# Products of constants between the masked scores of an attention stage

## The reference

```python
def _L3_gnn_ref(x, Wq, Wk, Wv, Wo, edge_index):          # 4 heads of 8
    src, dst = (edge_index[0], edge_index[1])
    q = (x @ Wq).reshape(N, N_HEADS, D_HEAD)
    k = (x @ Wk).reshape(N, N_HEADS, D_HEAD)
    v = (x @ Wv).reshape(N, N_HEADS, D_HEAD)
    scores = jnp.einsum('ehd,ehd->eh', q[dst], k[src]) * inv_sqrt_d
    m = jax.ops.segment_max(scores, dst, num_segments=N)
    e = jnp.exp(scores - m[dst])
    denom = jax.ops.segment_sum(e, dst, num_segments=N)
    msg = jax.ops.segment_sum(e[:, :, None] * v[src], dst, num_segments=N)
    attn_out = msg / jnp.maximum(denom, 1e-16)[:, :, None]
    return x + attn_out.reshape(N, N_HEADS * D_HEAD) @ Wo
```

## Time and profile before

| | us |
|---|---|
| median of 3 runs | 4871.88 |
| lowest, highest run | 4849.11, 4895.27 |
| span of the profiled execution, first to last instruction | 4857.7 |
| TensorE matmul busy | 2328.2 (48%) |
| VectorE busy | 1913.1 (39%) |
| ScalarE busy | 475.2 (10%) |
| GpSimd busy | 2571.2 (53%) |

### The profile page before, as it was taken

The page is one execution under the profiler, slowest core; times in us unless marked ns, Lnnn a source line. Parts: engine busy times, 40 slices in busy tenths (PEclk is TensorE's granted clock), DMA queues, the critical chain, the costliest instruction groups (busy, mean ns, idle before and its releaser), DMA issues. The chain is left out here.

```text
span 4857.7 us, 64843 instructions
## 1 busy us (share of the span) xinstructions
PE 2328.2 (48%) x20169; PEld 1793.5 (37%) x20302; DVE 1913.1 (39%) x6164; ACT 475.2 (10%) x1072; POOL 2571.2 (53%) x2544
## 2 busy tenths in 40 slices
PE   1300002332363232335556489888888455565562
PEld 0100002333343332334555355555555344344441
DVE  8000001111121111144545466665665455555557
ACT  0000000000000000000000022222222111111110
POOL 4777775666626666644554444444443444444440
PEclk9555555555555555555656699999998556656655
DMA  3211111000020000010000100000000000000010
GB/s 89 62 7 7 7 7 48 12 11 12 11 72 12 11 11 12 12 19 14 15 15 14 12 9 8 8 8 7 8 7 5 19 15 15 16 14 16 15 15 4
DMA packets 122759, 82.94 MB, mean 17 GB/s; under 512 B 75092, under 2 KB 109016, under 8 KB 122456
## 3 DMA queue, kind: packets, MB, share of 16 engines
q0 software_dynamic: 80160, 46.17, 8.2%
q1 hardware_dynamic: 42552, 36.17, 2.6%
HBM read 54.41 MB, written 27.29 MB: 17 GB/s over the span
## 5 line engine op out<-in xcount | busy, mean ns | idle before, releaser
L598 POOL DMA_INDIRECT rel_rows<-message_table,rel_index x880 | 842.5, 957 | 519.0 <-issue 277.0
L630 PE MATMUL rel_acc<-rel_rows,rel_onehot 128*128 128x32 f32 x1760 | 393.6, 372 | 872.4 <-issue 582.9
L630 PEld LDWEIGHTS rel_acc<-rel_rows,rel_onehot 128*128 128x128 f32 x1760 | 402.5, 324 | 863.5 <-issue 863.2
L1002 POOL DMA_INDIRECT flow_x<-node_table,flow_index x440 | 424.6, 965 | 548.5 <-DVE flow_index L1017 440.4
L1357 POOL DMA_INDIRECT att_kv_rows<-kv_table,att_index x440 | 421.0, 957 | 508.9 <-DVE att_index L1368 380.3
L362 POOL DMA_INDIRECT sorted_edges<-scatter_rows,scatter_index x425 | 505.4, 1189 | 131.7 <-issue 128.8
L1139 PE MATMUL flow_acc_bwd<-flow_onehot_j,flow_by_q 128*128 128x309 bf16 (+1 forms) x2508 | 557.5, 337 | 8.8 <-issue 0.4
L798 POOL DMA_INDIRECT sum_rows<-node_table,sum_index x320 | 326.3, 1020 | 295.1 <-DVE sum_index L821 195.6
L609 DVE COPY rel_index<-message_indices 128x8 uint32 x110 | 22.2, 202 | 1051.7 <-remote 956.1
L860 PE MATMUL p_sum_picked<-sum_h_parts,sum_source_onehot 128*128 128x96 bf16 x3000 | 250.6, 260 | 209.7 <-issue 204.1
L831 DVE TENSOR_SCALAR sum_source_onehot<-sum_sources,sum_node_numbers 128x384 bf16<-128x384 f16 x1000 | 235.7, 314 | 289.1 <-PE p_sum_picked L860 148.8
(11 more groups left out here) (248 smaller groups left out, 3861.8 us busy)
## 6 DMA issues: line engine op xcount, KB each, us to landing
message_table<-message_rows SPq DMA_DIRECT2D x50, 320.0 KB, 2.1
rel_rows<-message_table,rel_index POOLq DMA_INDIRECT x880
flow_x<-node_table,flow_index POOLq DMA_INDIRECT x440
att_kv_rows<-kv_table,att_index POOLq DMA_INDIRECT x440
sorted_edges<-scatter_rows,scatter_index POOLq DMA_INDIRECT x425
sum_rows<-node_table,sum_index POOLq DMA_INDIRECT x320
sorted_edges<-records SPq DMA_DIRECT2D x1, 4400.0 KB, 12.0
records<-sorted_edges SPq DMA_DIRECT2D x1, 4400.0 KB, 13.1
```

Source lines behind the costliest of these rows:

```text
L598: pool.indirect_dma_start(out=rows[b][:, t, :], out_offset=None, in_=table, in_offset=bass.IndirectOffsetOnAxis(ap=ibuf[b][:, t:t + 1], ax ...
L630: last = pe.matmul(acc[:, bass.ds(col, F)], hot[b][:, t, :], rows[b][:, t, :], start=False, stop=True, skip_group_check=True)
L1002: pool.indirect_dma_start(out=X[b][:, t, 0:F], out_offset=None, in_=d["nodes"], in_offset=bass.IndirectOffsetOnAxis(ap=ibuf[b][:, t:t + 1] ...
```

## The change

A function stay_busy issues one product on constants: the moving operand is 256 columns of att_pick, the stationary one the first 96 rows of the bfloat16 identity, and the result goes to the bank of p_att_parts, at times at which nobody reads that bank. No instruction waits for it, and it waits for no other engine. In each step it is called 15 times: after every masked_scores and before every one but the first.

```diff
+                    def stay_busy():
+
+                        pe.matmul(pP[:].bitcast(F32)[:, 0:BANK // 2], s["identb"][0:3 * G * HEADS, :], pick[:, 0:2, :],
+                                  start=True, stop=True, skip_group_check=True)
+
...
                     def step(i, k):
                         for t in range(G // 2):
+                            if t:
+                                stay_busy()
                             stage(masked_scores, i, k, 2, t)
+                            stay_busy()
                             if t == G // 2 - 1:
                                 stage(pick_maxima, i, k, 3)
                             stage(pick_q, i, k, 1, (2 * t, 2 * t + 1))
                         for t in range(G // 2, G):
+                            stay_busy()
                             stage(masked_scores, i, k, 2, t)
+                            stay_busy()
                             if t == G // 2 + 1:
                                 stage(turn_onehots, i, k, 0)
                         stage(add_up, i, k, 3)
```

## The result

The changed kernel took 4963.53 us (median of five runs, 4958.92 to 4997.24), the kernel before 4871.88. The ratio is 1.0206, 95% interval 1.0167 to 1.0245: slower, by 92 us in the medians, where 143 were forecast. The time lies inside the range. The profiled run is the slowest of the five (4997.24, span 4995.4); against the profiled span before it is 137.7 us longer, and 16 of those lie in stages that the change does not touch, ahead of the attention stage, whose first gather starts at 3821.6 instead of 3805.4. From its first to its last gather that stage takes 1037.5 us instead of 920.9, 117 more.

The account below looks back on a forecast made before the run. Bound: a ring of waits in the attention stage, with TensorE's signals held while gathers run. 52 steps at +2.78 us give +145 on the 4857.7 us span, 5002; plus 14 for timed runs, about 5015 us, range 4865 to 5080.

Parts of the forecast that it names:

- What bounds the kernel: Attention stage: no engine is full; a ring of waits of 16.6 us, 11.5 of them the gathers and the hold.
- The cliff: Attention step: pick_maxima ending 2.40 instead of 2.15 us after the first gather puts the next gathers at 19.72, not 16.58.
- the hold: Attention stage: TensorE's signals are held back while gathers run; att_gap follows pick_maxima by 5 us instead of 0.03.
- (1): Each added 256-column product takes TensorE 0.21 us at 1.2 GHz, 0.11 at 2.4; 3.2 or 1.7 us a step.
- (2): Seven products ahead of pick_maxima's signal: it ends 3.7 us after the first gather at half clock, 1.8 to 2.35 at full.
- (3): Four products between turn_onehots and add_up: first mask product only 1.35 us ahead of gathers, so late steps make late steps.
- (4): Four products between pick_maxima and turn_onehots: idle time, no cost; if products trickle, 0.85 us on the path.
- (5): Full clock on TensorE ends pick_maxima 0.63 us earlier and shortens transposes; taken as hidden and counted as nothing.
- The sum: Attention stage: 52 steps at 19.72 instead of 16.94 us, +145 us, about 5015 us in all, +3.0%; chance 0.50.
- No change: Rival: full clock before the first mask product keeps steps at 16.6 us; 4872, up to 10 more; chance 0.22.
- faster: Rival: clock stays at 2.4 GHz, TensorE's work on the ring shortens 1.2 us a step, 62 us: 4810; chance 0.11.
- Slower still: Rival: everything behind the hold trickles and four products come on the path, 20.7 us a step: about 5068; chance 0.17.

Follow-up runs that it names:

- e1: Kernel before plus only the seven added products between the first mask product and pick_maxima, on the first chip: 4032.82 us, ratio 1.002.
- e4: Kernel before, no product added, VectorE's index copy moved ahead of the split of the maxima so gathers start earlier, on the first chip: 4023.45 us, ratio 1.0004.
- f2: Kernel before plus four 512-column products, all ahead of turn_onehots, on a chip with late signals: 4812.73 us, ratio 1.0014.
- f1: The whole change again, unaltered, against the kernel before on the same chip: 4915.01 against 4801.32 us, ratio 1.0216.
- g1: Kernel before plus only the seven added products ahead of pick_maxima, on a chip with late signals: 4853.93 us, ratio 1.0121.
- g2: Kernel before plus only the last eight added products, from behind pick_maxima to add_up, on a chip with late signals: 4890.65 us, ratio 1.0213.
- g3: Kernel before, no product added, index copy ahead of the split of the maxima so gathers start earlier, on a chip with late signals: 4848.81 us, ratio 1.0099.
- g4: Changed kernel with VectorE's one-hots moved ahead of att_gap: 4852.05 us, ratio 1.012 to the kernel before.
- h1: Kernel before, no product added, with VectorE's one-hots moved ahead of att_gap: 4912.5 against 4877.55 us, ratio 1.007.
- e2: Kernel before plus only the last eight added products, from behind pick_maxima to add_up, on the first chip: 4025.33 us, ratio 1.0009.
- e3: Kernel before plus four 512-column products, all ahead of turn_onehots, on the first chip: 4026.57 us, ratio 1.0013.

## Why the prediction was right, and where its size was off

**What bounds the kernel: right.** The signals are held while gathers run one behind the other, but not within GpSimd's pause, and not at all in the first set of runs (e1 to e4).

**The cliff: right in effect, a staircase in fact.** It was put between 2.15 and 2.40 us for the end of pick_maxima. The traces of before and f2 have 90 regular steps; 83 of them by the start of its last product, 0.17 us ahead of its end (the other seven are earlier):

```
last product of pick_maxima   steps   att_gap: least / median / most   next gathers, mean
+1.5 to +1.8                   18      7.07 /  7.21 /  8.64            16.51
+1.8 to +2.1                   34      5.67 /  7.20 / 10.75            16.65
+2.1 to +2.4                   20      7.09 /  8.63 / 11.47            17.43
+2.4 to +3.0                    4     10.66 / 11.37 / 11.44            19.20
above +3.0                      7     11.35 / 11.48 / 12.06            19.47
```

The signal comes mostly at 7.1, 7.8, 8.6, 9.9, 10.7 or 11.4 us (in five steps at 5.7). Up to 8.7 us a later signal costs next to nothing, since the gathers bound the step, at 16.5 us in the mean; beyond 9.5 the next gathers stand 7.97 us behind att_gap (standard deviation 0.2; before, after, f1, f2, g1 and g2 agree within 0.03), 7.40 in g3, whose indices come earlier, 6.95 in g4 and h1 with the one-hots out of the way. And att_gap is at 11.3 to 11.7 us in most late steps, 1.7 us behind the end of the last gather (9.7): the hold lasts little longer than the gathers. So a late step costs up to 2.9 us and hardly more, which is the ceiling that g1 and g2 show.

**(1) The price of a product: right, and beside the point.** At 2.4 GHz the next product starts 0.11 us behind an added one, at 1.2 GHz 0.22 (taken: 0.11 and 0.21). f2, e2 and e3 show no such price in the time, and e1 at most 0.4%.

**(2) Seven ahead of pick_maxima: right in kind.** Forecast from the first mask product to the end of pick_maxima: 4.4 to 4.9 us at full clock; the step above has 4.35 (just below, at the lower price of issue alone). Alone (g1) they decide by the clock, as written: late at half clock, over the edge or not at full.

**(3) Four between turn_onehots and add_up: right, and the larger part.** Forecast: first mask product 1.35 us ahead of the gathers; measured 1.33 in the step above, 1.44 in the mean, 1.44 with the last eight alone, which cost the whole 2.1%. That the late state feeds itself holds: 47 of 47 regular steps are late. The four steps with GpSimd's pause take 15.4 to 18.3 us, which the prediction did not look at.

**(4) Four in the idle time: right for usual steps (f2).** In late ones they trickle with the rest, the case that the prediction named. No run took them apart there; h1 shows that work behind the held signal can delay it, but the signal of a late step is at its ceiling already.

**(5) The clock counts nothing: wrong in g1, right for the whole.** The full-clock share of the stretch from the first mask product to pick_maxima rose from 0.39 to 0.67, and with the last eight in place no clock saves the step.

**The sum: the term that was mis-sized is 52 x (19.72 - 16.94).** It took one late step, that of the earlier trace rows, for all. A late step measured 19.53 in the mean, 19.42 in f1, and the four steps with GpSimd's pause are shorter; 52 steps average 19.16, so the term is 52 x 2.22 = 115 us and not 145 in the profiled runs, and 52 x (18.96 - 16.97) = 103 between f1 and f2, on one chip, where the timed medians stand 102 apart. The stage was put at about 1010 us and took 985. The timed medians stand 92 apart and not 138 like the profiled spans, since the profiled run of the changed kernel was its slowest, 34 us above its median, and the profiled span before lay 14 us below its own; 16 us of the 138 lie ahead of the stage.

**The rivals.** No change and faster both fell: the clock did rise, and neither left the steps at 16.6 us nor shortened them. Slower still fell too: 20.7 us a step was put on products on the path behind the signal, and the ceiling forbids it. By the Trainium skill, page "SBUF — State Buffer", section "Who interferes with whom", TensorE waits on nobody, said there of SBUF's ports, which would have made the sum zero: the chip without the hold agrees (4025.33 against 4026.43 us with the last eight), the others do not (4890.65 against 4800.92).

**What stays open.** What the hold is. The last three sets of runs were made on three chips that have it, the first on one that has not, with the same kernel before; each set ran on one chip, so a cause in the set and not in the chip is not excluded. TensorE's products trickle in it and its signals are late, while VectorE's signals to TensorE are prompt (in h1 the first transpose starts 0.06 us behind the last one-hot, gathers running). That products and signals move on the same grid of 0.7 us suggests one cause for both, and no run tells whether it is TensorE's supply of instructions, its signals, or something that both share. Whether the gathers' descriptors or their data do it was not tried either. The pause of 1.67 us points at GpSimd's unbroken row of gathers, and a kernel that pauses behind the first gather of every group, or whose gathers start behind pick_maxima, would test it and might be faster than the kernel before; neither was run.

## What to carry to other kernels

Filler work on an engine is not free because its results are: look at which signal stands behind it, and at what that signal races against. Here work of the same kind (2048 columns a step) costs nothing in a hole that no signal crosses, and 1 to 2% ahead of a signal that the gathers cut off (1792 or 2048 columns); the reordering that only made gathers earlier cost 1% too. Where a time jumps, find the ceiling and the slack on both sides of the jump before multiplying by the number of steps, and time such a change on more than one chip.

## What was not expected of the hardware

The same kernel before takes 4871.88, 4801.32, 4800.92 and 4877.55 us in four sets of runs, and 4026.43 in a fifth: 16 to 17% less, on a chip where TensorE's signals pass while gathers run. That the hold makes the whole difference is not shown, for the other stages were not taken apart. From the first to the last gather the stages take 1338, 620, 933 and 921 us on the one and 1180, 455, 816 and 554 us on the other, there in the trace of e4 (the lines 598, 798, 1002 and 1357 of the gathers); the first stage with gathers (line 362) takes 632 or 633 on both.

The delay of a held signal moves in steps of about 0.7 us, and is not set by what is ahead of it alone (h1). A pause of 1.67 us in the row of gathers lets it through within 0.1 us.
